# Graph network step on one core: each batch's placing product in its own step, the last nodes' input products early, row scaling on GpSimd

## What is computed

```python
agg = segment_sum(edge_attr, dst, num_segments=6250)      # 106250 x 128 -> 6250 x 128
h   = relu(concatenate([x, agg, u[batch]], 1) @ W1 + b1)   # batch is all zero: u's part is a constant
out = h @ W2 + b2 + x
y   = layernorm(x + out)                                   # over 128 features, eps 1e-5
```

## Time and profile before

| what | value |
|---|---|
| time, median of 3 runs | 185.44 us (185.32 to 185.79) |
| the profiled execution | 185.73 us, of which 184.0 us are the span of its trace |
| granted PE clock over the span | 0.994 |
| busy share PE, DVE, ACT, POOL | 84, 63, 28, 14% |
| HBM traffic | 58.50 MB read, 3.20 MB written |

### The profile page before, as it was taken

The page is one execution under the profiler, slowest core; times in us unless marked ns, Lnnn a source line. Parts: engine busy times, 40 slices in busy tenths (PEclk is TensorE's granted clock), DMA queues, the critical chain, the costliest instruction groups (busy, mean ns, idle before and its releaser), DMA issues.

```text
span 184.0 us, 5378 instructions
## 1 busy us (share of the span) xinstructions
PE 154.1 (84%) x2195; PEld 113.9 (62%) x2195; DVE 115.4 (63%) x369; ACT 51.5 (28%) x110; POOL 25.4 (14%) x29
## 2 busy tenths in 40 slices
PE   0056979979979979969979999899889799899970
PEld 0046855955955956845846858467458568677850
DVE  6847499568376385485495466954933745877371
ACT  2021233223323313313313343133133241233230
POOL 7800030110200200200200204002003230000000
PEclk9999999999999999999999999999999999999997
DMA  5999999999999999999999999999999999998011
GB/s 119 315 352 373 374 375 373 371 373 374 374 374 373 375 372 373 376 372 373 374 373 374 375 373 374 375 373 360 363 374 374 371 374 370 367 398 303 11 43 33
DMA packets 42196, 62.07 MB, mean 337 GB/s; under 512 B 1975, under 2 KB 39541, under 8 KB 42170
## 3 DMA queue, kind: packets, MB, share of 16 engines
q1 hardware_dynamic: 41046, 61.23, 95.0%
q10 hardware_dynamic: 1124, 0.48, 1.2%
HBM read 58.50 MB, written 3.20 MB: 335 GB/s over the span
## 4 chain that ended last, share of the span: by engine, by line
PE 44%; DMA 39%; SPq 8%; DVE 4%; ACT 1%; issue 1%; DVEq 0%
DMA edge_ring<-in_edge_attr_dram 37%; PE sum_ps L845 17%; PE turn_ps L867 7%; PE hid_ps L907 6%; PE hid_ps L900 6%; PE out_ps L920 5%; SPq L276 4%; SPq L291 3%; DMA base_row<-in_dst_dram 2%; DVE bases L568 2%; PE xt_ps L920 1%; PE xt_ps L882 1%; DVE local_rows L576 1%; ACT local_t L429 1%; PE xt_ps L834 1%
## 5 line engine op out<-in xcount | busy, mean ns | idle before, releaser
L845 PE MATMUL sum_ps<-edge_ring,onehot 128*32 128x128 f32 x1662 | 58.5, 284 | 13.0 <-DMA edge_ring<-in_edge_attr_dram 10.8
L845 PEld LDWEIGHTS sum_ps<-edge_ring,onehot 128*32 128x32 f32 x1662 | 45.2, 113 | 27.9 <-DMA edge_ring<-in_edge_attr_dram 13.3
L630 DVE TENSOR_TENSOR agg_t<-agg_t,turn_ps 128x128 f32 x70 | 20.2, 288 | 56.7 <-PE turn_ps L867 52.6
L594 DVE TENSOR_TENSOR onehot<-iota,local_t 128x768 f32<-128x768 f32 (+1 forms) x40 | 33.6, 843 | 3.0 <-ACT local_t L429 2.4
L402 POOL TENSOR_TENSOR x_all<-x_all,half_b 128x512 f32<-128x512 f32 (+3 forms) x16 | 17.7, 1115 | 127.4 <-PE xt_ps L882 127.4
L466 ACT ACTIVATE hid_t<-hid_ps,bias 128x512 f32<-128x512 f32 (+3 forms) x32 | 18.1, 584 | 37.1 <-PE hid_ps L907 37.1
L867 PE MATMUL turn_ps<-place,sums 128*128 128x128 f32 (+1 forms) x140 | 26.5, 306 | 0.0
L907 PE MATMUL hid_ps<-agg_t,w_a 128*128 128x512 f32 (+3 forms) x64 | 24.1, 500 | 0.6 <-DVE agg_t L630 0.5
L867 PEld LDWEIGHTS turn_ps<-place,sums 128*128 128x128 f32 (+1 forms) x140 | 18.9, 192 | 8.0 <-issue 7.9
L920 PE MATMUL out_ps<-w_sb,hid_t 128*128 128x128 f32 (+1 forms) x176 | 21.9, 275 | 0.0
L441 ACT COPY sums<-sum_ps 128x256 f32<-128x256 f32 (+2 forms) x40 | 13.6, 341 | 25.9 <-PE sum_ps L845 25.9
(11 more groups left out here) (64 smaller groups left out, 73.0 us busy)
## 6 DMA issues: line engine op xcount, KB each, us to landing
edge_ring<-in_edge_attr_dram SPq DMA_DIRECT2D x69, 768.0 KB, 12.1
x_all<-in_x_dram SPq DMA_DIRECT2D x10, 256.0 KB, 10.5
out_dram<-x_all SPq DMA_DIRECT2D x1, 2304.0 KB
dst_rows<-in_dst_dram SPq DMA_DIRECT2D x1, 384.0 KB
x_all<-in_x_dram SPq DMA_DIRECT2D x1, 384.0 KB, 11.1
out_dram<-x_all SPq DMA_DIRECT2D x3, 128.0 KB
out_dram<-x_all SPq DMA_DIRECT2D x1, 256.0 KB
w_x<-in_L_gnn_W_dram ACTq DMA_DIRECT2D x1, 128.0 KB, 5.9
```

The source lines that it names most:

```text
L594: nc.vector.tensor_tensor(onehot[0:ROWS, b % BUFFERS, 0:k * TILES], cols, loc, ALU.is_equal).then_inc(onehot_ready, 1)
L630: nc.vector.tensor_tensor(to, to, turn_ps[b % 2][:, i * SPAN:(i + 1) * SPAN], ALU.add).then_inc(group_added, 1)
L845: last = nc.tensor.matmul(bank[c * WIN:(c + 1) * WIN], onehot[0:p, b % BUFFERS, i * TILES + c * R + r], edge_ring[0:p, slot, c * R + r], s ...
```

## The change

Five things move together.

1. `sum_ps` and `turn_ps` have one bank each, and `turn_batch(b)` stands in step b itself, behind `sum_batch(b)`. Between the two stands what the step has: a hidden or an out product, and in some steps nothing. The two banks freed are `keep_ps`.
2. The x half of piece n goes a step ahead of its a half. For the late pieces x is loaded with groups 2 to 8, transposed in steps 3, 5 and 6 and multiplied in steps 5, 6 and 7. For A and B the product is kept in SBUF (`x_hid_late`) and DVE adds it to the a half later (`add_x_hidden`); for the others it stays in PSUM until the a half comes.
3. The late pieces are A, B, C_ of 256, ODD of 106, E and END of 128, and their `complete_at` is 60, 64, 66, 67, 68, 70.
4. POOL scales the rows of LAST, A, B, C_ and ODD (`scale_rows`), not DVE.
5. `onehot` and `place` have 5 buffers and are made up to 5 batches ahead; `add_batch(b)` stands at the head of DVE's step b, and `norm_step(n, 0)` in the step of the out product.

```diff
-BUFFERS = 3
+BUFFERS = 5
+AHEAD = 5
+COMPLETE_AT = [6, 12, 18, 24, 30, 36, 40, 46, 52, 58, 60, 64, 66, 67, 68]
+LATE_LOAD_AT = [2, 3, 4, 5, 7, 8]
+LATE_TURN_STEP = [3, 5, 6]
+LATE_SUM_STEP = [5, 6, 7]
...
+    y_step = out_step
+    moments_step = [o + (n < LAST) for n, o in enumerate(out_step)]
+    root_step = [m + 1 for m in moments_step]
+    scale_step = root_step
+    pool_scaled = range(LAST, E)
+    made_by = [min(b + 3 + sum(hidden_step[n] <= b for n in range(AHEAD - 2)), n_batch) for b in range(n_batch)]
+    hidden_x_step = [max(h - 1, turns[turned_at[n]][0] + 1) for n, h in enumerate(hidden_step[:n_big])]
...
+            def scale_rows(n):
+                _, p, j = pieces[n]
+                pool.wait_ge(rstd_ready, n + 1)
+                for slot in range(x_slot[n], x_slot[n] + j):
+                    last = nc.gpsimd.tensor_scalar(x_all[0:p, slot], x_all[0:p, slot], mean_var[0:p, slot, 0:1],
+                                                   rstd[0:p, slot:slot + 1], ALU.subtract, ALU.mult)
+                last.then_inc(late_normalized, 1)
...
+            def add_x_hidden(n):
+                dve.wait_ge(hidden_summed, m_chunks * (n + 1))
...
+                for m in range(m_chunks):
+                    xh = x_hid_late[:, m, late_cols(n)]
+                    nc.vector.tensor_tensor(xh, hidden_bank(n, m), xh, ALU.add).then_inc(late_added, 1)
...
+            for b in range(n_batch):
...
+                add_batch(b)
+                for m in range(made_by[b - 1] if b > 0 else 2, made_by[b]):
+                    make_onehot(m)
+                    make_place(m - 1)
...
             def turn_batch(b):
                 pe.wait_ge(batch_copied, b + 1)
                 pe.wait_ge(place_ready, b + 1)
-                if b >= 2:
-
-                    pe.wait_ge(group_added, batch_first[b - 1])
+                if b > 0:
+
+                    pe.wait_ge(group_added, batch_first[b])
...
             def sum_out(n):
...
+                if 0 < n <= A:
+
+                    pe.wait_ge(y_ready, n)
...
-            for b in range(late_step):
+            for b in range(n_batch):
                 sum_batch(b)
-                if b > 0:
-                    turn_batch(b - 1)
+                for n in range(n_pieces):
+                    if n < n_big and hidden_x_step[n] == b:
+                        sum_hidden_x(n)
+                    if hidden_step[n] == b:
+                        sum_hidden_a(n)
+                for n in range(END):
+                    if out_step[n] == b and n not in range(B, E):
+                        sum_out(n)
+                turn_batch(b)
+                for n in range(B, E):
+                    if out_step[n] == b:
+                        sum_out(n)
```

More of the change, by code:

```diff
@@ L57, in gnn_resnorm_kernel @@
     half = BLOCK // 2
[L58 to L61, removed]
+    odd0 = late0 + 3 * half
+    odd_nodes = n_nodes - odd0 - 2 * P
+    odd_cut = odd_nodes // 16 * 16
+    assert 0 < odd_nodes < P
     pieces = [(b * BLOCK, P, J) for b in range(n_big)]
     pieces += [(late0 + h * half, P, J // 2) for h in range(3)]
-    pieces += [(rest0 - 2 * P, P, 1), (rest0 - P, P, 1), (rest0, rest_nodes, 1)]
+    pieces += [(odd0, odd_nodes, 1), (n_nodes - 2 * P, P, 1), (n_nodes - P, P, 1)]
     n_pieces = len(pieces)
-    A, B, C_, D, E, REST = range(n_big, n_pieces)
+    A, B, C_, ODD, E, END = range(n_big, n_pieces)
     LAST = n_big - 1
@@ L69, in gnn_resnorm_kernel @@
     x_slots = sum(p[2] for p in pieces)
-    complete_at = [6, 12, 18, 24, 30, 36, 40, 46, 52, 58, 60, 63, 66, 67, 69, n_grp]
+    complete_at = COMPLETE_AT + [n_grp]
     assert len(complete_at) == n_pieces
[L74 to L80, removed]
+    least_at = [(complete_at[n], pieces[n + 1][0]) for n in range(n_pieces - 1)]
+    batch_first = list(range(0, SINGLE0, PAIR)) + list(range(SINGLE0, n_grp)) + [n_grp]
     n_batch = len(batch_first) - 1
@@ L327, in store, with wait_scaled @@
                     sp.dma_start(to[cut:p], src[cut:p]).then_inc(stored, 16)
-            sp.wait_ge(normalized, LAST)
+            def wait_scaled(n):
+                if n in pool_scaled:
+                    sp.wait_ge(late_normalized, n - pool_scaled.start + 1)
+                else:
+                    sp.wait_ge(normalized, sum(m not in pool_scaled for m in range(n + 1)))
+            wait_scaled(LAST - 1)
             store(0, LAST)
             for n in range(LAST, n_pieces):
-                sp.wait_ge(normalized, n + 1)
+                wait_scaled(n)
                 store(n, n + 1)
@@ L733, in _ @@
[L733 to L748 removed]
+                for n in range(END):
+                    if y_step[n] == b:
+                        norm_step(n, 0)
+                    if moments_step[n] == b:
+                        norm_step(n, 1)
+                        norm_step(n, 2)
+                    if scale_step[n] == b:
+                        norm_step(n, 3)
+                        if n not in pool_scaled:
+                            norm_step(n, 4)
@@ L750, in _ @@
+            norm_step(E, 3)
+            norm_step(E, 4)
+            for step in range(5):
+                norm_step(END, step)
             general = dve.value_load(flag[0:1, 0:1], min_val=0, max_val=1)
@@ L998, in _ @@
+            sum_hidden_a(END)
+            sum_out(END)
             pe.wait_ge(flag_ready, 1)
```

451 lines of the change are left out of this document (209 added, 242 removed).

## The result

The changed kernel takes **180.87 us** (median of 4 runs, 180.81 to 181.12), beside 185.47 us of the kernel before in the same comparison: a ratio of 0.9752 [0.9735, 0.9769]. A second comparison gave 180.78 against 185.57. The profiled execution took 180.84 us, its span 179.1, its mean granted clock 0.989.

The account below looks back on a forecast made before the run. PE's work after 144.55 us bounds the kernel: 27.7 us to END's a half plus 6.45 us give 178.7, with POOL's hold 179.2, profiled 180.9, median forecast 180.7 us; range 178.6 to 183.2.

Parts of the forecast that it names:

- PE's own work: PE from group 59's sum to the last placing product: sums, placing products, a halves and out products, 24.2 us.
- bare copies, steps 32, 33, 35: Steps where nothing stands between sum and placing product, so the copy is exposed: 3 x 0.53 = 1.6 us.
- y of LAST ahead of A's out product: Step 31: A's out product uses LAST's bank and waits for DVE's y of LAST, costing 1.1 us.
- last add: At the very end nothing hides DVE's add, so END's a half starts later: 0.5 us.
- 0.1 for the pair step before: Before group 59's sum, work moved ahead of it makes PE 0.1 us late.
- POOL's 0.5: Late steps: POOL's scaling, 0.3 to 0.5 us a slot, holds DVE's onehot and place and delays B's a half 0.5 us.
- DVE isn't on the path there but for the two waits named: Last stage: ridding DVE of 11 scalings of 0.35 us was given no gain, though one was not excluded.
- margin of 0.6 us: Around steps 32 to 34: DVE is 0.6 us ahead of the deadline for the add that B's a half needs.
- From there the chain is PE alone: Kernel before, 144.55 to 175.65 us: the chain is only PE's work, 31.1 us long.
- No lock: Rival, late steps: POOL holds nothing and there is no wait for y; 179.1 us, chance 0.08.
- The hard lock: Rival, late steps: each of LAST's and A's six scalings on POOL holds DVE; 182.3 us or more, chance 0.15.
- The lost cover: Rival, pair steps: copies become exposed and PE falls behind from about 30 us; up to 187 us, chance 0.05.

Follow-up runs that it names:

- experiments 1: Changed kernel with the x products of A and B, C_, E and half of END back in steps 29, 31 and 32: 183.93 us, ratio 0.9894.
- Experiment 6: Changed kernel with A's out product a step later, in step 32 instead of 31: 180.37 us, ratio 0.9704.
- experiment 8: Changed kernel with A's out product in step 32, B's in step 36, and B's relu behind the copy of step 35: 180.06 us, ratio 0.9701.
- experiment 3: Changed kernel without POOL's scaling, the rows of LAST to ODD stored as y: 180.95 us, ratio 0.9737.
- experiment 4: Changed kernel with the scaling of LAST, A, B, C_ and ODD back on DVE: 183.59 us, ratio 0.9856.
- experiment 5: Changed kernel with POOL's scaling written as two tensor_tensors with broadcast mean and rstd: 181.31 us, ratio 0.9768.
- experiment 2: Changed kernel with the x halves of pieces 1 to 8 back in their a half's step: 182.37 us, ratio 0.982.
- experiments 9 to 11: Kernel before without late x products, 0.9939; then also add ahead of onehot and place, 0.9964; then also DVE scaling one column of LAST to D, 0.9943.

## Why the prediction was right, step by step

**The stage and the mechanism.** What PE does after 144.55 us was what counted; experiments 1 and 6 move the time by what they move on PE there. From group 59's sum to END's a half, forecast and trace of after:

| term | forecast us | measured us |
|---|---|---|
| start of group 59's sum (shift from 144.55) | 0.1 | 0.5 |
| PE's own work | 24.2 | 24.4 |
| bare copies, steps 32, 33, 35 | 1.6 | 0.46 + 0.46 + 0.71 = 1.6 |
| steps 37 to 39 | 0.2 | 0 |
| y of LAST ahead of A's out product | 1.1 | 1.0 |
| last add | 0.5 | 0.47 |
| POOL's hold on DVE | 0.5 | 0 |
| END's a half to the end of the span | 6.45 | 6.5 |

The measured own work is what is left of 172.57 - 145.05 = 27.5 us (the row of the pair's sums starts at 144.26; group 59's start is taken 0.79 later) once the four waits below it, 3.1 us, are taken off. A bare copy costs more than its idle 0.39: sum to placing product is 1.18 instead of 0.79, and the placing product then takes 0.49 instead of 0.42, since nothing runs ahead of it. In step 35 the wait is longer, and the profile names DVE's `place` as what ended it:

```profile
161.85 0.24 ACT L524 COPY sums<-sum_ps 128x128 f32<-128x128 f32 x1
162.14 0.49 PE L923 MATMUL turn_ps<-place,sums 128*128 128x128 f32 x2 [0.65 <-DVE place L675]
```

But by the program the places made there are those of steps 38 and 39, and the copy ends at 162.09, as far ahead of the placing product as in steps 32 and 33. The releaser was ACT, as forecast. The copy is late because the relu of B (160.97 to 161.94), which waits for DVE's `add_x_hidden`, stands ahead of it on ACT; with that relu behind the copy (experiment 8) the wait is 0.39, and the placing product starts before those places do. The prediction had no such term.

**Two terms were mis-sized, and cancel. That the forecast of 180.7 came within 0.2 us is in part luck.** The first is "0.1 for the pair step before". The prediction and the account of the change place all of the late x's products in steps 5 to 7, but those of ODD and half of END stand in step 28 (0.67 us), after PE's last wait for edges; group 59's sum is 0.5 late. The second is "POOL's 0.5". POOL was slower than thought, 0.79 us a slot and not 0.3 to 0.5, and held nothing (experiment 3). The rule cited from the Trainium skill, "SBUF — State Buffer", section "SBUF: two separate sides", counts any GpSimd instruction as a holder; by this trace the tensor_scalar form with a column of mean and of rstd does not hold an onehot (0.55 and 0.57 beside it; a place took 0.39 instead of 0.28), while the tensor_tensor form does (1.41). The measurement decides.

**Two sentences were wrong.** "DVE isn't on the path there but for the two waits named": with LAST's four scalings on DVE, 1.12 us, the kernel is 1.4 to 2.8 us slower (experiment 4). That is more than the margin of 0.6 us that I gave DVE, and the path goes from A's statistics over ACT's root to the copy of step 33, which the prediction did not look at. "From there the chain is PE alone": in the kernel before it holds the wait of 0.48 us at 160.83, which is most of the 0.7 us that the list of PE's work (30.4 of 31.1) had left.

**Rivals.** No lock: true by experiment 3, but with the y wait in place the time is 180.9, not 179.1. The hard lock needs another instruction form, and even the form that holds gave 181.31 us, not 182.3 (experiment 5). The lost cover is real in kind (experiment 2), and the slack that protects from it is almost used up: PE's last wait for edges ends at 136 us, where the kernel before still waited at 144. In the windows of after (each engine's busy us) PE is behind from 50 to 70 us and waits again before 110, as forecast; that it is busy throughout once more from 110 to 130 was not forecast. It follows a step with both halves of a piece (106.18 and 108.00 us), where `COMPLETE_AT` leaves four groups between two pieces (36 and 40) and not six; that this is the cause was not tested:

```profile
50.00:70.00 20.00, 20.00 (x311) 15.25 (x310) 15.94 (x42) 5.62 (x10) 2.58 (x2) 1.00 1.06 374
...
90.00:110.00 20.00, 17.75 (x244) 11.91 (x244) 12.21 (x30) 6.11 (x11) 2.57 (x2) 1.00 1.06 374
110.00:130.00 20.00, 20.00 (x313) 15.29 (x313) 16.57 (x48) 6.55 (x12) 2.59 (x2) 1.00 1.06 374
```

**Better than both.** Experiment 6 (0.9704) beats the kernel before and the changed one; experiment 8 is level with it.

## What to carry to other kernels

Work that stands in a compute-bound tail is worth close to its full length if it can go where the same engine waits for a stream, and the sum of idle time there says how much fits. Taking work from one engine's tail gains only what the other engine's list allows: look for who stands ahead of the instruction that it waits for (experiments 9 to 11), and move that too. When a buffer loses its second bank, price each wait as idle time plus the longer instruction behind it, and put the products that are free to move over the bare copies.

## What the runs showed of the hardware

- An idle 1.5 us of PE, with 5.05 of 6 and 1.43 of 2 us busy before it, was followed by 3.4 us at 1.2 GHz in one kernel; a sum took 1.51 instead of 0.86 (experiment 4). By their mean clocks two of the kernel's six runs had no such stretch.
- On POOL a tensor_scalar with two columns as scalars takes 0.79 us for 128x128; two tensor_tensors with broadcast operands take 1.04 us each for 128x512. Only the second form held DVE's onehot (1.41 us instead of 0.55, experiment 5; 0.55 and 0.57 beside the first).
- The hold works both ways: POOL's 128x256 tensor_tensor took 1.05 us where it met an onehot, and 0.61 where it didn't (experiment 5). Of the changed kernel's tensor_scalars one took 1.16 us instead of 0.79, the one that started with an onehot (158.95 and 158.96 us).
